# Where the DC column is symmetrised: half of the images behind the large product

## The reference

```
x = x + conv3x3(gn(x))
x = x + column_scan(gn(x))       # a gated recurrence over the 64 columns
x = x + low_modes(gn(x))         # rfft2, 16 x 16 modes times complex weights, irfft2
x = x + all_modes(gn(x))         # below
```

```
x_ = rfftn(x, s=(64, 64))                   # 64 x 33 complex modes per channel and image
y_ = einsum('oihw,bihw->bohw', kernel, x_)  # a 32 x 32 complex matrix for each mode
y  = irfftn(y_, s=(64, 64)) + bias
```

## Time and profile before

| | us |
|---|---|
| median of 3 runs | 582.54 |
| lowest and highest | 581.66 and 582.75 |
| profiled execution | 583.71 |
| its span in the trace | 581.9 |

### The profile page before, as it was taken

The page is one execution under the profiler, slowest core; times in us unless marked ns, Lnnn a source line. Parts: engine busy times, 40 slices in busy tenths (PEclk is TensorE's granted clock), DMA queues, the critical chain, the costliest instruction groups (busy, mean ns, idle before and its releaser), DMA issues.

```text
span 581.9 us, 28732 instructions
## 1 busy us (share of the span) xinstructions
PE 531.0 (91%) x11428; PEld 419.8 (72%) x11428; DVE 473.1 (81%) x1270; ACT 392.7 (67%) x832; POOL 298.0 (51%) x424
## 2 busy tenths in 40 slices
PE   3999999699999999999999999998878997999995
PEld 2333333477777777777777899997667986899995
DVE  7678885569898989898989778879976898477876
ACT  2445979867777777777777968765748997566441
POOL 7565664046666666666666322005658889320100
PEclk9999999979999999999999999999999999999999
DMA  6910000011111111111111400000307887203325
GB/s 212 397 21 0 2 2 5 1 43 44 38 44 37 45 36 45 36 45 36 45 36 37 146 3 2 0 1 3 110 17 236 268 277 225 67 1 147 145 107 184
DMA packets 26043, 45.80 MB, mean 79 GB/s; under 512 B 5632, under 2 KB 16128, under 8 KB 25104
## 3 DMA queue, kind: packets, MB, share of 16 engines
q1 hardware_dynamic: 24912, 44.98, 24.4%
q10 hardware_dynamic: 672, 0.15, 0.1%
q0 software_dynamic: 416, 0.07, 0.1%
HBM read 28.53 MB, written 8.39 MB: 63 GB/s over the span
## 4 chain that ended last, share of the span: by engine, by line
PE 40%; DVE 33%; issue 11%; ACT 8%; POOL 3%; DVEq 2%; DMA 2%; SPq 0%; POOLq 0%; ACTq 0%
PE psum L654 14%; PE psum L683 8%; DVE spec L1364 7%; DVE spec L1356 5%; PE psum L858 5%; DVE spec L1367 5%; PE psum L815 4%; DVE small L1249 3%; PE psum L934 3%; PE psum L782 2%; POOL work L377 2%; ACT work L300 2%; ACT work L377 2%; PE psum L718 2%; DVE spec L1359 2%
## 5 line engine op out<-in xcount | busy, mean ns | idle before, releaser
L718 PE MATMUL psum<-spec,matrices 128*32 128x128 f32 x3024 | 110.0, 279 | 14.1 <-ACT spec L1051 7.3
L718 PEld LDWEIGHTS psum<-spec,matrices 128*32 128x32 f32 x3024 | 76.7, 110 | 45.9 <-ACT spec L1051 45.8
L725 PE MATMUL psum<-spec,matrices 128*32 128x128 f32 x3024 | 107.8, 275 | 0.9 <-DMA spec<-work 0.9
L566 POOL TENSOR_TENSOR spec<-spec 64x128 f32<-64x128 f32 x126 | 70.6, 561 | 72.3 <-DVE spec L1367 72.3
L725 PEld LDWEIGHTS psum<-spec,matrices 128*32 128x32 f32 x3024 | 85.8, 111 | 4.1 <-issue 3.5
L683 PE MATMUL psum<-spec,matrices 128*64 128x512 f32 x384 | 87.2, 611 | 1.0 <-ACT spec L985 1.0
L858 PE MATMUL psum<-work 128*32 128x128 f32 x2368 | 70.1, 274 | 9.8 <-POOL work L377 4.1
L858 PEld LDWEIGHTS psum<-work 128*32 128x32 f32 x2368 | 63.4, 110 | 16.4 <-issue 15.0
L544 POOL TENSOR_SCALAR spec<-image,small 32x960 f32<-32x960 f32 (+1 forms) x48 | 55.5, 1157 | 35.2 <-PE psum L683 22.7
L560 POOL TENSOR_TENSOR image<-image,spec 128x128 f32 (+1 forms) x128 | 69.3, 542 | 0.0
L683 PEld LDWEIGHTS psum<-spec,matrices 128*64 128x64 f32 x384 | 27.3, 140 | 54.3 <-issue 51.3
(11 more groups left out here) (152 smaller groups left out, 854.2 us busy)
## 6 DMA issues: line engine op xcount, KB each, us to landing
work<-w_dram SPq DMA_DIRECT2D x66, 256.0 KB, 3.5
spec<-work SPq DMA_DIRECT2D x124, 64.0 KB, 1.9
image<-x_dram SPq DMA_DIRECT2D x3, 2048.0 KB, 11.8
out_dram<-image SPq DMA_DIRECT2D x3, 2048.0 KB, 7.0
image<-x_dram SPq DMA_DIRECT2D x4, 512.0 KB, 6.0
work<-w_dram SPq DMA_DIRECT2D x1, 2048.0 KB, 7.8
out_dram<-image SPq DMA_DIRECT2D x4, 512.0 KB, 2.9
kept<-const_dram SPq DMA_DIRECT2D x1, 192.0 KB, 5.1
```

Source lines behind the costliest of these rows:

```text
L566: nc.gpsimd.tensor_tensor(straddled(h, ROWS_01, 0), *of, ALU.subtract).then_inc(lower_ready[h], 1)
L718: last = mm(psum[QUARTERS[hm], 4 * h + g, 0:HB], sv[:, g, QUARTERS[hm]], moving[hm], start=starts, stop=True)
L725: last = mm(psum[q, 4 * h + g, 0:HB], sv[:, 3 + g, q], e, start=True, stop=stops)
```

## The change

GpSimd keeps five of its ten symmetrisation instructions between the steps (steps 20 to 24: ri = 1, images 0 to 7), and the vector engine five of its own (ri = 0, images 0 to 7). The other ten, both parts of images 8 to 15, stand on GpSimd behind step 32, one after the other, with its own buffer `t_pool` for the sums of both parts. TensorE waits for five on each counter before the transposes of images 0 to 3. GpSimd waits for five of the vector engine's and all 15 of its own before it stages images 8 to 11.

```diff
--- before.py
+++ after.py
@@ -618,17 +618,21 @@
                     pool.wait_ge(mix_done, s_ - 2)
                 for m in (2, 3):
                     spread(nc.gpsimd.tensor_copy, s_, m).then_inc(spread_pool, 1)
-                if 20 <= s_ < 30:
+                if 20 <= s_ < 25:
                     k = s_ - 20
                     if k == 0:
                         pool.wait_ge(nyq_moved, 8)
                         pool.wait_ge(y_moved, NCHUNK // 2)
                     else:
                         pool.wait_ge(sym_pool, k)
-                    symmetrise_step(nc.gpsimd.tensor_tensor, 1, k // 5, t_pool, k % 5).then_inc(sym_pool, 1)
+                    symmetrise_step(nc.gpsimd.tensor_tensor, 1, 0, t_pool, k).then_inc(sym_pool, 1)
+
+            for k in range(10):
+                pool.wait_ge(sym_pool, 5 + k)
+                symmetrise_step(nc.gpsimd.tensor_tensor, k // 5, 1, t_pool, k % 5).then_inc(sym_pool, 1)
             pool.wait_ge(y_moved, NCHUNK)
-            pool.wait_ge(sym, 10)
-            pool.wait_ge(sym_pool, 10)
+            pool.wait_ge(sym, 5)
+            pool.wait_ge(sym_pool, 15)
             with pool.Fori(2, NG) as j:
                 pool.wait_ge(a_done, j * 8)
                 nc.gpsimd.tensor_copy(ystage.rearrange("p (n b) -> p n b", b=GB),
@@ -918,8 +922,8 @@
                 if first:
                     src = spec[:, :].rearrange("p (g k r q b) -> p g k r q b", g=2, k=H, r=2, q=4)
                     pe.wait_ge(nyq_moved, 8)
-                    pe.wait_ge(sym, 10)
-                    pe.wait_ge(sym_pool, 10)
+                    pe.wait_ge(sym, 5)
+                    pe.wait_ge(sym_pool, 5)
                 else:
                     src = ys
                     pe.wait_ge(ystaged, j + 1)
@@ -1550,13 +1554,13 @@
                     dve.wait_ge(y_moved, NCHUNK // 2)
                 else:
                     dve.wait_ge(sym, k)
-                symmetrise_step(v.tensor_tensor, 0, k // 5, t_sum, k % 5).then_inc(sym, 1)
+                symmetrise_step(v.tensor_tensor, 0, 0, t_sum, k).then_inc(sym, 1)
 
             for s_ in range(STEPS):
                 scale_chunk(s_)
                 if s_ >= 3 and s_ != 7:
                     move_y(s_ - 3)
-                if 20 <= s_ < 30:
+                if 20 <= s_ < 25:
                     symmetrise(s_ - 20)
             for s_ in range(STEPS - 3, STEPS):
                 move_y(s_)
```

## The result

| | before | changed | ratio, 95% interval |
|---|---|---|---|
| first comparison, median (4 and 4 runs) | 582.63 | 578.45 (577.97 to 579.89) | 0.9936 (0.9919 to 0.9953) |
| profiled execution, span | 583.71, 581.9 | 579.89, 578.1 | |

The change makes the kernel faster, by 4.2 us between these medians; 2.5 were forecast, 580.0 us, and 578.45 lies 0.55 under the range's low end of 579.0. By the interval the gain is between 2.7 and 4.7 us.

The account below looks back on a forecast made before the run. GpSimd, late from mix 25 on through its symmetrisations, bounds the product; eight mixes at 1.90 us take 15.2 instead of 17.74, the tail costs nothing, so 582.54 less 2.5 gives 580.0 us, range 579.0 to 581.8.

Parts of the forecast that it names:

- GpSimd is the bound from mix 24 or 25 on: Large product: GpSimd's reserve is used up at mix 24; from there each symmetrisation delays TensorE in full, 2.22 us a step.
- Mix 25 still starts at 484.50: Large product: steps 20 to 24 stay as they are, so mix 25's start should not move, within 0.3 us.
- GpSimd goes on at 1.74 a step, and TensorE is the last again at once: Behind mix 25: GpSimd's copies take 1.74 us a step, so TensorE becomes the last, by 0.1 us at first.
- Eight mixes at 1.90: Mixes 25 to 32 on TensorE: 15.2 us at 1.90 each against 17.74, a gain of 2.5 us.
- 1.80 (7.20 / 4): Fastest pace considered, from mixes 0 to 3: mixes 25 to 32 in 14.4 us, a gain of 3.3 us.
- The tail is hidden: GpSimd's ten instructions behind step 32, 6.0 to 6.8 us, fit into its 18.88 us idle time before L634 and cost nothing.
- Rival 3: At the product's end, GpSimd's tail slows the vector engine's copies, costing 0.4 to 1.5 us: 580.4 to 581.5; chance 0.10.
- 20 us of tail, and each microsecond beyond puts L634 off by one: Behind step 32: GpSimd's wait covers a tail up to 20 us; each further us delays staging copy L634 by one.
- rivals 1 and 2: Mixes 25 to 32 wait for weights: gain gone, 581.6 to 582.8 us, chance 0.09; or slower, 583.8 us, chance 0.05.
- Rival 4: In the product, the scalar or vector engine replaces GpSimd as bound: 2.05 us a step, 581.2 us; chance inside the forecast's 0.76.
- Two steps in hand: Large product: GpSimd starts step 20 with about two steps of reserve, used up at mix 24.
- The Trainium skill's rule on the shared port: Vector instructions with two SBUF inputs and GpSimd instructions reading SBUF lock each other out: L412 took 0.75 us instead of 0.40.

Follow-up runs that it names:

- the two halves: Edits of the changed kernel: only GpSimd's five instructions moved behind step 32, 579.48 us; only the vector engine's five moved there, 582.36 us.
- the later runs: The changed kernel timed again without any edit, two more times beside the kernel before: 579.34 and 579.64 us.
- the tail of 50: The changed kernel with 40 more GpSimd instructions of the same form and size behind the ten after step 32: 591.98 us.
- Halved weights: The changed kernel with weight transfers of half the size from step 6 on, so the product is partly wrong: 578.90 us.
- the vector engine's half alone: The changed kernel with GpSimd's ten instructions back between the steps, only the vector engine's last five moved to GpSimd behind step 32: 582.36 us.

## Why the prediction was right in direction and short in size

**GpSimd is the bound from mix 24 or 25 on**: right, and shown by the two halves.

**Mix 25 still starts at 484.50**: its place among the steps held (0.59 us late, by GpSimd, behind the fifth instruction), its time came 0.9 us earlier, outside the 0.3 that the prediction allowed. Of that, 0.6 was there before the product began.

**GpSimd goes on at 1.74 a step, and TensorE is the last again at once**: right, 1.755.

**Eight mixes at 1.90**: the step that failed, a term of the sum that was mis-sized. The changed kernel's profiles have 14.83, 14.53 and 14.92 us, 1.82 to 1.87 a step, against 15.2. The true gain of this term is 2.8 to 3.2 us, not 2.5. That is 0.3 to 0.7 of the 1.7 us by which the first comparison went beyond the forecast; 0.3 more came from mixes 0 to 24, and the rest is not a matter of this term (see the range). The row of mixes 12 to 16 was the wrong neighbour: in it the scalar engine had used up its lead by the Nyquist copies, which mixes 25 to 32 don't have. The other row, 13.26 us for seven mixes, was taken as free of waits, though the last of those seven waits for GpSimd, by 0.2 us in the changed kernel. A row that was named, and used only as a bound, was the right one: the last three mixes at 5.50 / 3 = 1.83, a stretch where GpSimd had no symmetrisation, no Nyquist copy ran and TensorE had no gap, exactly the state that the change makes of the other five. It gave 579.4 as the time, in the range and close to the 579.34 and 579.64 of the later runs.

**The range**: its fastest case, "1.80 (7.20 / 4)", was misread. TensorE's rows of the product, of which the earlier trace rows shows most, add up to 2112 = 33 x 64 matmuls, so no record is missing, and the row of 251 is 5 short of four mixes; whole mixes start 1.76 us apart there. Below that case the range went 0.2 us for everything outside the product. But over the 14 profiles of this study the product's first matmul lies between 432.18 and 433.43 us, with the same instructions ahead of it in all. With 0.6 us of that on its low side, the range would hold 578.45. A median moves less than one execution, though: the four of the kernel before lie within 0.2 us. Why the first comparison's median lay 0.9 to 1.2 us below the two later ones stays open.

**The tail is hidden**: right. 6.76 us, 495.8 to 502.6 (496.5 to 503 forecast), 12.6 us of idle time left, no time back without it. Rival 3 falls with that.

**"20 us of tail, and each microsecond beyond puts L634 off by one"**: right for L634 by the run with the tail of 50, but for the kernel's end the point is about 10 us later, where the copy is late for the transposes.

**Weights**: rivals 1 and 2 fall. Halved weights leave mixes 25 to 32 at 14.56, and the waits on which both rivals rested fall at counts of matmuls where none for weights can be. The prediction's sign for late weights, "issue" as releaser, was the wrong one: the one wait for weights that was found is booked as a DMA. But DMA moved 229 GB/s from 484.5 to 497, not the 270 to 280 forecast: the last transfers are asked for three steps ahead, so they are over before the product is (53 GB/s from 495 to 499).

**Rival 4**, the vector or scalar engine next in line: not behind mix 25. The release of mix 24, booked on the scalar engine in the earlier trace rows, was GpSimd's in the trace: the scalar engine's copies had ended 1.90 us before, GpSimd's 0.24. But the scalar engine was the last by mixes 16 and 17, where the pace was read off.

**Two steps in hand**: by the trace of the kernel before, GpSimd's copies of step 20 ended 1.82 us before mix 20, one step's time; 1.21, 0.88 and 0.24 us were left at mixes 21, 22 and 23.

**The Trainium skill's rule on the shared port** spoke for a hidden price of the vector engine's L412. It is real as a duration: in the kernel before the vector engine's L407 and L412, both inputs in SBUF, took 0.40 to 0.88 us, and each of the four ended 0.26 to 0.28 us after the GpSimd instruction that ran when it started. So the 0.40 at 474.33, too, stood beside a GpSimd copy, but one that ended 0.13 us later. Taking these instructions away bought nothing: with the vector engine's half alone the time is the same.

## What to carry to other kernels

An instruction put between the steps of a pipeline costs its full length on the engine that is nearest to the bound, once its reserve is used up, and nothing measurable on one with reserve; which it is shows in whose work ends just before the bound engine starts, and moving one engine's half at a time proves it. The releaser that a row names can be one that was long done, as for mixes 23 and 24. For the pace after the bound is gone, take the stretch whose other engines have the same work as the stretch in question, here the three steps right behind it, and not the one that is longest or averages more. And a reserve of 1.8 us is used up by a run of additions on one engine; spaced apart they cost less (one wait of 0.58 us was left), and on an engine that has time they cost nothing that a row shows: with images 0 to 7 on the vector engine the kernel takes 577.3 us, with the Nyquist copies shared as well 577.0, 2.6 less than the changed kernel beside it.

## What the runs showed of the hardware

TensorE's clock falls in a wait and costs after it. In the run with the tail of 50, TensorE idled for 9.65 us up to 539.27; the granted clock was 0.66 from 530 to 540 and 0.83 from 540 to 550, so part of the time at 1.2 and not 2.4 GHz. The 32 transposes behind the wait took 5.70 us where they take 3.87 at full clock: 1.8 us on top of the wait.

Executions of one code differ by a microsecond ahead of the product, and the clock is one reason. The same first 60 matmuls of the convolution, in the profile of before:

```profile
13.81 16.11 PE L683 MATMUL psum<-spec,matrices 128*64 128x512 f32 x60
```

and of the changed kernel:

```profile
13.69 14.88 PE L687 MATMUL psum<-spec,matrices 128*64 128x512 f32 x60
```

They are 1.23 us apart, with DMA at 382 and 383 GB/s from 13 to 30 us. The first of these matmuls come in pairs 0.85 us apart, the later ones in pairs 0.43 us apart, which is the ratio of the levels of 1.2 and 2.4 GHz. The trace's clock record begins, at full clock, at 19.90 us in the kernel before and at 17.32 in the changed one (the 1.00 that a window shows ahead of that is not a reading), and the kernel before takes seven of the long steps, the changed kernel four: three more at 0.42 us each are 1.26 us. Over the 14 profiles this record begins between 16.44 and 19.90 us. By the product's start 0.57 of the 1.23 us is left. Whether the clock also made three executions of the first comparison fast can't be said, since they left no trace.
